# The mixing's fifth normaliser, scaling and transposes, one chunk of products later

## What is computed

```python
xn = layernorm(x)
x  = x + gnn(xn, edge_attr, coeffs, src, dst, paths) + mix(xn)
x  = x + ffn(layernorm(x))
# gnn: for each edge, 64 products coeff * xn[src][seg i1] * edge[seg i2], summed into seg i3 of node dst
# mix (linear attention, 8 heads): k', q' = elu(.)+1;  z = (q' @ (k'^T v)) / (q' . sum(k') + 1e-6);  z @ W_out + b
# ffn: 2 shared experts and 6 of 64 routed experts for each node, SwiGLU
```

## Time and profile before

| | us |
|---|---|
| three executions, median (lowest to highest) | 1015.66 (1013.46 to 1018.88) |
| profiled execution, its own time | 1019.58 |
| profiled execution, span from first to last instruction | 1017.5 |
| busy in the span: TensorE | 895.9 |
| busy in the span: VectorE | 548.1 |
| busy in the span: ScalarE | 256.0 |
| busy in the span: GpSimd | 268.2 |

### The profile page before, as it was taken

One profiled execution on the slowest core, in us unless ns is written; L12 is line 12 of the kernel. 1 busy time (PEld: TensorE's weight loads), 2 busy tenths in 40 slices (PEclk: granted clock), 3 DMA queues, 4 the chain that ended last, 5 costly groups with the idle time before them and its releaser, 6 DMA issues. The chain is left out here.

```text
span 1017.5 us, 20833 instructions
## 1 busy us (share of the span) xinstructions
PE 895.9 (88%) x7497; PEld 589.3 (58%) x7497; DVE 548.1 (54%) x1623; ACT 256.0 (25%) x573; POOL 268.2 (26%) x265
## 2 busy tenths in 40 slices
PE   1599998897878298999999999999999989999991
PEld 1355555564544196676556566766676765656660
DVE  7997987978798986323324333334233332333216
ACT  2111101121130132333322322333233322322331
POOL 4543321334300102222222222222222322222211
PEclk9699999999989789999999999999999999999996
DMA  8856454565428951889979999999988999999976
GB/s 276 287 207 207 158 186 171 207 207 208 166 63 279 373 206 57 319 303 367 405 290 334 359 383 413 390 387 361 405 307 332 353 400 398 365 374 366 402 289 262
DMA packets 76929, 300.68 MB, mean 296 GB/s; under 512 B 13730, under 2 KB 14119, under 8 KB 58548
## 3 DMA queue, kind: packets, MB, share of 16 engines
q1 hardware_dynamic: 57256, 254.21, 65.9%
q0 software_dynamic: 17280, 38.48, 10.5%
q10 hardware_dynamic: 2252, 6.06, 1.7%
HBM read 290.26 MB, written 26.62 MB: 311 GB/s over the span
## 5 line engine op out<-in xcount | busy, mean ns | idle before, releaser
L1202 DVE TENSOR_TENSOR arena<-arena 128x288 f32 (+1 forms) x640 | 236.3, 449 | 37.8 <-remote 24.5
L1826 PE MATMUL bank<-arena,low 128*64 128x256 f32 x2048 | 241.6, 383 | 2.0 <-issue 2.0
L1667 PE MATMUL bank<-arena,multi 128*64 128x256 f32 x1296 | 162.0, 400 | 44.0 <-DVE arena L1202 32.6
L1826 PEld LDWEIGHTS bank<-arena,low 128*64 128x64 f32 x2048 | 141.0, 137 | 75.6 <-issue 12.4
L1851 PE MATMUL bank<-arena,low 128*64 128x256 f32 x1392 | 161.6, 379 | 1.1 <-ACT low L980 1.1
L1667 PEld LDWEIGHTS bank<-arena,multi 128*64 128x64 f32 x1296 | 99.5, 144 | 102.2 <-issue 44.2
L743 POOL DMA_INDIRECT low<-xr_d,idx x64 | 90.2, 1409 | 238.7 <-DVE place L1433 177.6
L747 POOL DMA_INDIRECT y_d<-low,place x64 | 68.5, 1070 | 262.3 <-ACT low L987 181.8
L1851 PEld LDWEIGHTS bank<-arena,low 128*64 128x64 f32 x1392 | 101.3, 137 | 50.3 <-ACT low L980 1.3
L987 ACT ACTIVATE low<-bank,gcol 64x256 f32<-64x256 f32 x174 | 82.1, 472 | 105.0 <-PE bank L1851 103.9
L687 POOL DMA_INDIRECT arena<-xn_d,ssel x79 | 90.3, 1143 | 38.2 <-issue 21.8
(11 more groups left out here) (214 smaller groups left out, 710.9 us busy)
## 6 DMA issues: line engine op xcount, KB each, us to landing
arena<-in_L_ffn_Wg_dram SPq DMA_DIRECT2D x64, 1024.0 KB
arena<-in_L_ffn_Wu_dram SPq DMA_DIRECT2D x64, 1024.0 KB
arena<-in_L_ffn_Wd_dram SPq DMA_DIRECT2D x64, 1024.0 KB
arena<-in_edge_attr_dram SPq DMA_DIRECT2D x88, 256.0 KB
arena<-y_d SPq DMA_DIRECT2D x5, 1250.0 KB, 6.8
sums_d<-arena ACTq DMA_DIRECT2D x18, 256.0 KB, 3.2
arena<-sums_d SPq DMA_DIRECT2D x4, 896.0 KB
arena<-in_L_mix_W_qkv_dram SPq DMA_DIRECT2D x2, 1024.0 KB, 18.1
```

The source lines that it names most:

```text
L1202: return dve.tensor_tensor(prod[:, buf, 0:n, EXT * p:EXT * p + EXT], x1[b][:, 0:n, bass.ds(i1, EXT)], x2[b][:, 0:n, bass.ds(i2, EXT)], ALU ...
L1667: ins = pe.matmul(bank[2 * b + c // 2][64 * h:64 * h + 64, 256 * (c % 2):256 * (c % 2) + 256], pair[:, pairs, i, :], prod[:, buf, i, 256 * ...
L1826: ins = pe.matmul(out_bank[64 * h:64 * h + 64, w * HF:(w + 1) * HF], xgT[:, b, k, 64 * o:64 * o + 64], gu[:, slot, w, k, h * HF:(h + 1) * HF],
```

## The change

One entry of one list:

```diff
         MIX = (24, 25, 28, 29, 32)
-        MIXED = (27, 28, 31, 32, 34)
+        MIXED = (27, 28, 31, 32, 35)
```

## The result

| | before | changed |
|---|---|---|
| median of 12 executions | 1016.73 us | 1021.3 us |
| lowest to highest | 1013.46 to 1024.25 | 1016.01 to 1024.22 |
| profiled execution, span | 1017.5 us | 1019.3 us |

The ratio is 1.004, with a 95% interval of 1.0023 to 1.0056. The change made the kernel slower by 4.6 us at the median (2.3 to 5.7 us by the interval), where a gain of 3.7 us was forecast. The measured time lies above the forecast range, which ended at 1016.8 us. Medians and ratios in this document leave out two slow executions, of 3160.13 and 4217.65 us, one each in two of the experiments.

What follows compares the result with a forecast made beforehand. VectorE was taken to pace the edited edges stage, TensorE the experts. Profiled: 1019.58 - 4.1 = 1015.5 us; median: 1015.66 - 3.7 = 1012.0 us. The range reached almost down to 1008.6 us and up to 1016.8 us.

Steps and rivals of the forecast that it cites:

- The three waits and their order: VectorE, 255 to 350 us: 4.1 us for `mix_values`, 3.7 us for sums read back, 1.5 us ahead of chunk 33.
- the normaliser's wait would vanish: VectorE in chunk 33: its 16 products run without a stop in 5.99 us, and VectorE gains 4.1 us.
- nothing is lost on TensorE: TensorE runs chunk 33 without idle time ahead; the 0.59 us of transposes behind chunk 35 are hidden.
- exactly 3.4 us would come between chunk 35 and the flush: ScalarE's queue: transposes, copy and `clear_top`, 0.6 + 0.58 + 2.19 us, stand ahead of `flush(8)`, where there was no delay.
- the path sums begin when the last read lands: VectorE's products would end at 313.5 us, so the read back of the last tile stays the last to arrive.
- the stages behind shift as a block: Layer norm, routing and experts move together with the earlier end of the edges stage, 4.1 us in the profiled execution.
- Rival 2: ScalarE's queue: store follows its issue, 2.4 us wait removed against 3.4 us added; slower, 1016.7 us; chance 0.10.
- Does that store matter?: Window 8's store is held by the 4 MB read, lands at 311.1 us, and the whole 4.1 us is kept.
- The bound at the other end: If the 12.45 us are the store's own, path sums begin at 320.6 us and only 0.7 us is kept.
- I expect these two to swap, which costs nothing net: VectorE's gaps of 0.80 us behind the chunk with the normaliser and 0.47 us behind the next trade places.
- the removed wait: VectorE's wait of the fifth normaliser for `mix_values`, taken near 4.1 us from the profile.
- the bound for a faster chunk 32: TensorE at full clock in chunk 32 ends `mix_values(4)` 1.7 us sooner, leaving a removable wait of 2.4 us.

Runs made afterwards that it cites:

- the third comparison: The unchanged edit measured a third time against the kernel before, on a chip where before takes some 1017 us: 1018.07 us, ratio 1.0014.
- 36: The change with 36 in place of 34 as fifth entry of MIXED, against the kernel before: 992.76 us, ratio 0.9935; once more 1014.92 us, ratio 0.9983.

## Why the prediction was wrong

**What held.** The three waits and their order; that the normaliser's wait would vanish; that nothing is lost on TensorE; that exactly 3.4 us would come between chunk 35 and the flush; that the path sums begin when the last read lands; and that the stages behind shift as a block. Rival 2 named the mechanism, its place and the point from which it decides: a removed wait under 3.4 us. It was given 0.10, and its 1016.7 us is still well under what was measured.

**The step that failed** is "Does that store matter?". The prediction took the store's 12.45 us as the drain of the 4 MB read, put the 3.4 us in front of the flush at nothing and kept the whole 4.1 us. It expected 17.7 us from the 4 MB read's issue to the last read's, and some 9 us for the store; they were 21.7 and 13.0 us. With the read issued 8.7 us ahead instead of 5.3 us, the store took 13.0, 12.7 and 12.2 us. Issued together with the read it still took 9.8 us. It did fall to 10.9 and 10.3 us where it was issued 9.2 and 10.3 us behind the read, so the read's drain has some part. Rows 9, from which the store was to be in after 5.3 us at most, had only 8 of 18 landings, mostly short ones. Rows 10 were right and proved less than was made of them: two packets in three microseconds say that the store was being held, not for how long it would be held in another order. The bound at the other end, a time fixed from the issue, was nearer.

The Trainium skill (DMA: Bandwidth & Descriptors, "Queues, rings and completion order") has the DMA engines take turns between queues with work, packet by packet. The trace of the change disagrees for the first 6.3 us after the store's issue, in which only the read's queue moved, and agrees from 310.7 to 317.4 us, when q10 moved 160 packets and q1 153.

**Two terms were mis-sized.** "I expect these two to swap, which costs nothing net": the gaps ahead of chunks 34 and 35 grew from 1.27 to 2.28 us together, and by 1.0 us again in the third comparison; at 998 us they grew by 0.3 us at most. The register load for chunk 35 now follows a chunk with a normaliser in it, and chunk 35 also waits for `s_turn`, which chunk 34 does not; that these make the gap was not tested. And the removed wait was taken as 4.1 us, because two chunks at the same place of a window had taken 5.79 us, with 2.4 us as the bound for a faster chunk 32; the profile taken beside the third comparison shows 2.0 us. Chunk 32 took 5.79 us in one of the 18 profiles, and 4.1 to 4.3 us in 15. Its pace is not the whole of it: in two of the profiles of before at 998 us chunk 32 took 4.11 us and the wait was still 4.0 us, as chunk 33 began there with no wait ahead of it. With 2.0 us removed, 1.0 us lost in gaps and 3.4 us put ahead of the flush, the store is issued 2.4 us later (29.5 against 27.1 us in the table). On top of that it took 1.2 us longer to land, and the last read 0.9 us longer. These add to the 4.5 us between 44.5 and 49.0 us. The medians of that comparison differ by only 1.2 us, so its pair of profiles, too, is one draw.

**What stays open.** Why the store's first packet needs about 6 us beside the read, and why its whole time was 12.2 to 13.0 us where the read was 8.7 us ahead and 10.3 us where it was 10.3 us ahead. What the "remote" wait ahead of chunk 33 is, which shows only in the profiles at 1017 us, was not tried either.

## What to carry over

When a step is moved past a queue, look for the transfer that is issued from that queue, and price its lateness at full size unless an experiment shows a shorter transfer. Before a median of landings is used as a price, count how many were matched: the 8 of 18 here were mostly the short ones. A wait read from one profile is one draw: the same wait was 2.0 to 5.4 us here, with chunk 32 at 4.1 to 5.8 us, and a change that trades it against a fixed cost of 3.4 us can come out on either side. Here the trade needn't be made: with 36, or with the flush ahead of the copy, the wait goes and the store isn't late, and 36 beat the change on both kinds of chip (992.8 us where before takes 998.5 us, 1014.9 against 1018.1 us at 1017 us; in the latter case its gain over before is not clear of noise).

## What was not expected of the hardware

A store of 512 KB, issued in two halves that at other windows land in about 7 us each at the median (profiles at 998 us), took 9.4 to 13.0 us beside a 4 MB read on another queue, and 9.8 us when both were issued within 0.1 us. And one and the same program takes 998 to 1000 us on three chips and 1017 us elsewhere; the difference lies ahead of chunk 33, which starts at 251 to 254 us or at 271 to 275 us. VectorE's "remote" waits up to 275 us add to 24.5 and 25.3 us in the two profiles of before at 1017 us, and the three of before at 996 to 999 us have none.
